# Local attention layers: half of the value windows used in place, tokens swapped on GpSimd, values and feed-forward part later

## What is computed

```python
def local_attention(q, k, v):            # 16 heads of 64, windows of 32 tokens
    bk2, bv2 = look(bk), look(bv)        # each window sees the one before and itself
    sim = einsum('bhwie,bhwje->bhwij', bq, bk2) * QK_SCALE
    attn = softmax(where(mask, -max, sim), -1)
    return einsum('bhwij,bhwje->bhwie', attn, bv2)
def attn_layer(x, Wqkv, qs, ksc, Wo):
    q, k, v = split(x @ Wqkv)            # q and k: l2norm, scale, rotary
    return local_attention(q, k, v) @ Wo
for i in range(6):
    x = attn_layer(shift_tokens(x), ...) + x
    x = ffn_layer(shift_tokens(x), ...) + x   # layernorm, W1, a * gelu(gate), W2
```

## Time and profile before

| | us |
|---|---|
| median of 3 runs | 2512.24 (2499.67 to 2514.59) |
| the profiled execution | 2506.73 |
| its span | 2504.8 |
| PE busy | 2354.9 |
| DVE busy | 1717.0 |
| ACT busy | 1597.2 |
| POOL busy | 1451.3 |

### The profile page before, as it was taken

How to read it: one execution, slowest core, us unless ns; L and a number is a source line. 1 busy time by engine, 2 the same in 40 slices (tenths; PEclk the granted TensorE clock), 3 DMA queues, 4 the chain that set the end, 5 groups by cost and what they waited for, 6 DMA issues and landing times.

```text
span 2504.8 us, 121652 instructions
## 1 busy us (share of the span) xinstructions
PE 2354.9 (94%) x53677; PEld 1748.5 (70%) x53677; DVE 1717.0 (69%) x3393; ACT 1597.2 (64%) x5036; POOL 1451.3 (58%) x1408
## 2 busy tenths in 40 slices
PE   9958999999999999999999999999888999999967
PEld 8836777777777777677777777777645666666657
DVE  4477788777888888787788788887335555555534
ACT  3226777777777787777777778777625454545422
POOL 1166667656676676566666677665117656656307
PEclk9969999999999999999999999999979999999978
DMA  4013333433333334333343333333216222222136
GB/s 91 15 33 86 79 83 94 97 80 83 91 93 95 82 83 103 83 92 87 80 96 90 80 92 87 87 87 87 54 30 177 49 48 48 48 48 48 31 97 249
DMA packets 230208, 204.60 MB, mean 82 GB/s; under 512 B 133687, under 2 KB 155464, under 8 KB 229552
## 3 DMA queue, kind: packets, MB, share of 16 engines
q1 hardware_dynamic: 225296, 190.91, 30.5%
q0 software_dynamic: 2208, 5.58, 0.7%
q10 hardware_dynamic: 2176, 0.33, 0.1%
HBM read 86.05 MB, written 15.70 MB: 41 GB/s over the span
## 4 chain that ended last, share of the span: by engine, by line
PE 66%; DVE 12%; SPq 6%; ACT 5%; issue 5%; POOL 4%; DMA 3%; POOLq 0%; ACTq 0%; DVEq 0%
PE psum L1211 7%; PE psum L1959 5%; PE psum L1237 5%; PE psum L1229 5%; PE psum L1938 4%; PE psum L1111 4%; PE psum L1944 3%; PE psum L1113 3%; PE psum L1112 3%; PE psum L1993 3%; PE psum L1983 3%; ACT p L1357 3%; SPq L972 3%; PE psum L1188 2%; PE psum L1219 2%
## 5 line engine op out<-in xcount | busy, mean ns | idle before, releaser
L1357 ACT ACTIVATE p<-p,stat 128x64 f32<-128x64 f32 x1536 | 512.4, 336 | 47.2 <-DVE stat L1491 44.9
L1577 POOL TENSOR_TENSOR p<-p,inverse 128x512 f32<-128x512 f32 x192 | 200.2, 1043 | 456.5 <-DVE inverse L1494 452.2
L1211 PE MATMUL psum<-kT,qT 32*32 32x64 f32 x24576 | 305.5, 224 | 25.8 <-issue 24.2
L2092 DVE TENSOR_REDUCE largest<-psum 128x1 f32<-128x512 f32 x256 | 165.0, 687 | 228.0 <-PE psum L1944 228.0
L1211 PEld LDWEIGHTS psum<-kT,qT 32*32 32x32 f32 x24576 | 264.1, 103 | 75.3 <-issue 74.3
L1357 ACT ACTIVATION_READ_ACCUMULATOR p<-p,stat 128x1 f32 x1536 | 288.6, 188 | 0.0
L1421 DVE SCALAR_TENSOR_TENSOR rotated<-psum,scales,rotary 128x512 f32<-128x512 f32 x384 | 270.8, 742 | 25.8 <-ACT sq L1293 25.8
L1556 POOL TENSOR_TENSOR squares<-sq 128x512 f32<-128x512 f32 x192 | 245.3, 1278 | 44.3 <-ACT sq L1293 43.8
L1293 ACT ACTIVATE sq<-psum 128x512 f32<-128x512 f32 x384 | 213.7, 582 | 57.3 <-PE psum L1113 54.6
L1229 PEld LDWEIGHTS psum<-pT,v_win 64*64 64x64 f32 x12288 | 198.6, 136 | 64.7 <-issue 45.9
L1111 PE MATMUL psum<-xs,wqkv_high 128*128 128x512 f32 x384 | 205.7, 536 | 23.2 <-DVE rotated L1421 22.9
(11 more groups left out here) (351 smaller groups left out, 5402.3 us busy)
## 6 DMA issues: line engine op xcount, KB each, us to landing
v_win<-v_tok SPq DMA_DIRECT2D x576, 128.0 KB
rnorm_wide<-rnorms SPq DMA_DIRECT2D x384, 64.0 KB
v_win<-v_tok SPq DMA_DIRECT2D x336, 64.0 KB
q_rows<-q_rows_all SPq DMA_DIRECT2D x32, 512.0 KB, 4.6
tile_weights<-expert_table SPq DMA_DIRECT2D x23, 512.0 KB, 5.8
wqkv<-L_ffn_Wqkv SPq DMA_DIRECT2D x96, 64.0 KB, 2.2
...
```

What stands on the lines that cost most here:

```text
L1211: last = PE.e.matmul(psum[WIN * blk:WIN * (blk + 1), f, out], q[rows, g, half, tok:tok + WIN], k[rows, g, half, tok:tok + 2 * WIN], start= ...
L1357: last = A.e.activation(p, p, ACT.Exp, bias=t.stat[:, h, 2 * g + f:2 * g + f + 1], accum_out=t.sum[:, h, g, f:f + 1])
L1577: G.e.tensor_tensor(p, p, t.inv[:, h, :, :].unsqueeze(3).to_broadcast([P, GROUPS_TF, 2, 2 * WIN]), ALU.mult).then_inc(*t.p_scaled.by(m))
L2092: V.e.tensor_reduce(t.mx[n % 4][:, :], psum[:, n % 5, :], AX, ALU.max, negate=True).then_inc(*t.largest.by(n))
```

## The change

Values. Windows 1 and 3 of a tile need the keys 0 to 63 and 64 to 127, which is how the copied values lie. `v_tok` goes; the copy writes slot 0 of `v_win`, used as it is for these two, and SP moves the data by 32 partitions into slot 1 for windows 0 and 2. So that f = 0 and f = 1 stay in different halves of the partitions, the tokens of the f = 1 values have their halves swapped: GpSimd makes a swapped copy `x_swapped` of the unit's tokens (two tensors, four copies of 128x256) at round 28, and the value matmuls of f = 1 use it. Score, weigh, mix and the norm copy follow that order; the norm copy becomes three instructions. DMAs per tile: 6 instead of 10 (4 instead of 8 in a unit's first). The value copy now waits for the weighing of the tile two before.

Schedule. Values from round 29 to 33, windows from 31 to 37, the whole feed-forward part four rounds later, the norms' row out at 19 instead of 15, wide norms at 20, 20, 26, 29 instead of 16, 18, 19, 24, and the loads of the next layer's weights two rounds later. The windows of a round now stand before its wide norms in SP's queue.

```diff
-VALUE_FIRST, WINDOWS_AT = 29, 31
+VALUE_FIRST, WINDOWS_AT, SWAP_AT = 33, 37, 28
...
-NORM_AT = {"root0": 17, "out": 15, "root1": 33, "turn": 39, "copy": 39}
-SPREAD_AT = (16, 18, 19, 24)
-SCALE_AT = (24, 28, 29, 32)
+NORM_AT = {"root0": 17, "out": 19, "root1": 33, "turn": 39, "copy": 39}
+SPREAD_AT = (20, 20, 26, 29)
+SCALE_AT = (24, 28, 31, 32)
-FFN_AT = {"shift": 80, "center": 83, "square": 84, "sum": 84, "root": 84, "spread": 88, "scale": 89, "gate0": 91, "gate1": 95, "gate2": 96, "gelu": 99,
-          "up0": 100, "up1": 101, "up2": 104, "down": 108, "add": 109}
+FFN_AT = {"shift": 84, "center": 87, "square": 88, "sum": 88, "root": 88, "spread": 92, "scale": 93, "gate0": 95, "gate1": 99, "gate2": 100, "gelu": 103,
+          "up0": 104, "up1": 105, "up2": 108, "down": 112, "add": 113}
...
+SPLIT_AT = {2: 13, 3: 31, 0: 39, 1: 40, 4: 60, 5: 62}
...
+                if s == PART_FIRST + PART * (PARTS - 1) + PART_STEPS + 1:
...
-            if s in SPREAD_AT:
-                norms_wide(c, t, u, SPREAD_AT.index(s))
             i, at = divmod(s - WINDOWS_AT, TILE)
             if 0 <= i < TPB and at == 0:
                 value_windows(c, t, u * TPB + i)
+            for g in range(GROUPS_TF):
+                if s == SPREAD_AT[g]:
+                    norms_wide(c, t, u, g)
     for v_in in t.v_in + t.wide_in:
...
+def swapped(f, blk):
+
+    return f if blk < TPB // 2 else 1 - f
...
+    w0, w1, w2, w3 = (slice(WIN * w, WIN * (w + 1)) for w in range(TPB))
+    SP.e.dma_start(v[WIN:P, 1, 0, :, :], v[0:P - WIN, 0, 0, :, :]).then_inc(*v_in.by((n, 0)))
+    SP.e.dma_start(v[w1, 1, 1, :, :], v[w0, 0, 1, :, :]).then_inc(*v_in.by((n, 1)))
+    SP.e.dma_start(v[w0, 1, 1, :, :], v[w3, 0, 1, :, :]).then_inc(*v_in.by((n, 2)))
+    SP.e.dma_start(v[w3, 1, 1, :, :], v[w2, 0, 1, :, :]).then_inc(*v_in.by((n, 3)))
+    if n % TPB:
+        SP.e.dma_start(v[w0, 1, 0, :, :], before[w3, 0, 0, :, :]).then_inc(*v_in.by((n, 4)))
+        SP.e.dma_start(v[w2, 1, 1, :, :], before[w1, 0, 1, :, :]).then_inc(*v_in.by((n, 5)))
...
+        if f:
+            PE.wait_ge(*t.swapped.on(u))
+        tokens = [x[:, i * P:(i + 1) * P] for x in (t.xp if f else xs)]
+        three_products(PE, ps, tokens, w).then_inc(*t.valued.by((u * TPB + i, f)))
...
+def mixed_rows(t, h, g):
+
+    ot = t.ot[h][:, g, 0:H64]
+    return bass.AP(ot.tensor, ot.offset, [list(ot.ap[0]), [P + H64 if g % 2 == 0 else H64 - P, 2], [1, H64]])
...
-                        last = PE.e.matmul(psum[WIN * blk:WIN * (blk + 1), f, out], q[rows, g, half, tok:tok + WIN], k[rows, g, half, tok:tok + 2 * WIN],
+                        last = PE.e.matmul(psum[WIN * blk:WIN * (blk + 1), swapped(f, blk), out], q[rows, g, half, tok:tok + WIN], k[rows, g, half, tok:tok + 2 * WIN],
...
-        PE.wait_ge(*t.v_in[n % 2].on((n, 9 if i else 7)))
+        PE.wait_ge(*t.v_in[n % 2].on((n, 5 if i else 3)))
         for a in range(2):
             for blk in range(TPB):
                 for o in range(2):
                     for f in range(2):
-                        rows, to, at = slice(DH * f, DH * f + DH), (f + o) % 2 * DH, a * P + blk * WIN
-                        last = PE.e.matmul(psum[to:to + DH, 2 + o, at:at + WIN], v[rows, blk, 2 * (2 * a + o) + h, :],
+                        slot, to, at = swapped(f, blk), (f + o) % 2 * DH, a * P + blk * WIN
+                        rows = slice(DH * slot, DH * slot + DH)
+                        last = PE.e.matmul(psum[to:to + DH, 2 + swapped(o, blk), at:at + WIN], v[rows, 1 - blk % 2, f, 2 * (2 * a + o) + h, :],
                                            t.pt[h][rows, 2 * a + o, blk * WIN:(blk + 1) * WIN], start=True, stop=True)
         last.then_inc(*t.weighted.by(m))
...
+def swap_halves(t, u, k):
+
+    to, x = (y[:, :].rearrange("p (i a q) -> p i a q", i=TPB, a=2) for y in (t.xp[k], t.xs[u % 2][k]))
+    return [(to[:, :, 1 - a, :], x[:, :, a, :]) for a in range(2)]
...
-        A.e.activation(t.rq[u % 2][:, :, :].rearrange("p b r -> p (b r)"), ring_bank(c, t, "unit", u, "rn")[:, 0:P], ACT.Copy).then_inc(*t.rn_kept.by(u))
+        norms = ring_bank(c, t, "unit", u, "rn")[:, 0:P]
+        A.e.activation(t.rq[u % 2][0:H64, :, :].rearrange("p b r -> p (b r)"), norms[0:H64, :], ACT.Copy)
+        pairs = lambda x: x.rearrange("p (b a h f g) -> p b a h f g", b=TPB, a=2, h=2, f=2)
+        for f in range(2):
+            last = A.e.activation(pairs(t.rq[u % 2][H64:P, :, :].rearrange("p b r -> p (b r)"))[:, :, 1, :, 1 - f, :], pairs(norms[H64:P, :])[:, :, 1, :, f, :], ACT.Copy)
+        last.then_inc(*t.rn_kept.by(u))
...
-        for m in (n - 2, n - 1):
-            if m >= 0:
-                A.wait_ge(*t.v_in[m % 2].on((m, 9 if m % TPB else 7)))
-        A.e.activation(t.vt[n % 2][:, f, :, 0:DH], ring_bank(c, t, "unit", u, f"v{i}{f}").rearrange("p (h d) -> p h d", d=DH), ACT.Copy).then_inc(*t.v_kept.by((n, f)))
+        if n >= 2:
+            A.wait_ge(*t.weighted.on(2 * (n - 2) + 1))
+        if n >= 1:
+            A.wait_ge(*t.v_in[(n - 1) % 2].on((n - 1, 5 if (n - 1) % TPB else 3)))
+        A.e.activation(t.v[n % 2][:, 0, f, :, :], ring_bank(c, t, "unit", u, f"v{i}{f}").rearrange("p (h d) -> p h d", d=DH), ACT.Copy).then_inc(*t.v_kept.by((n, f)))
...
+    if s == SWAP_AT:
+        if u:
+            G.wait_ge(*t.valued.on((u * TPB - 1, 1)))
+        for k in range(2):
+            for to, x in swap_halves(t, u, k):
+                last = G.e.tensor_copy(to, x)
+        last.then_inc(*t.swapped.by(u))
```

More of the change, by code:

```diff
@@ L726 @@
 TABLES = (2, 3, 0, 1)
-UNIT_STEPS = 110
-SPLIT_AT = {2: 13, 3: 31, 0: 39, 1: 40, 4: 56, 5: 59}
+UNIT_STEPS = 118
+SPLIT_AT = {2: 13, 3: 31, 0: 39, 1: 40, 4: 60, 5: 62}
 RAW = 2
@@ L790, in transformer_setup @@
     t.xs = [[sb(f"xs{i}_{k}", [P, S], F32R) for k in range(2)] for i in range(2)]
+    t.xp = [sb(f"x_swapped{k}", [P, S], F32R) for k in range(2)]
     t.xf = sb("x_ffn", [P, S])
@@ L799, in transformer_setup @@
     t.rq = [sb(f"rnorm_tok{i}", [P, TPB, 32]) for i in range(2)]
-    t.vt = [sb(f"v_tok{i}", [P, 2, PAIRS, DH]) for i in range(2)]
-    t.v = [sb(f"v_win{i}", [P, TPB, PAIRS, DH]) for i in range(2)]
+    t.v = [sb(f"v_win{i}", [P, 2, 2, PAIRS, DH]) for i in range(2)]
     t.stat, t.sum, t.inv = sb("stat", [P, 2, 2 * GROUPS_TF]), sb("sum", [P, 2, GROUPS_TF, 2]), sb("inverse", [P, 2, GROUPS_TF, 2])
@@ L819, in transformer_setup @@
     t.valued, t.v_kept = per("valued", tiles, halves), per("v_kept", tiles, halves)
-    t.v_in = [Signal(nc, f"tf_v_in{i}", [(n, k) for n in range(i, UNITS_TF * TPB, 2) for k in range(10 if n % TPB else 8)], 16) for i in range(2)]
+    t.v_in = [Signal(nc, f"tf_v_in{i}", [(n, k) for n in range(i, UNITS_TF * TPB, 2) for k in range(6 if n % TPB else 4)], 16) for i in range(2)]
     t.scored, t.scores_kept, t.biased, t.exped, t.inverted, t.p_scaled, t.turned, t.pt_kept, t.weighted, t.o_kept = (
@@ L828, in transformer_setup @@
     t.shift_high, t.shift_low = per("shift_high", units, halves), per("shift_low", units, halves)
+    t.swapped = one("swapped", units)
     t.tab_turned, t.tab_kept = one("tables_turned", TABLES), one("tables_kept", TABLES)
@@ L925, in transformer_sync @@
             if b == B - 1 and l + 1 < DEPTH:
-                if s == PART_FIRST + PART * (PARTS - 1) + PART_STEPS - 1:
+                if s == PART_FIRST + PART * (PARTS - 1) + PART_STEPS + 1:
                     SP.wait_ge(*t.mixed.on((u + 1) * TPB - 1))
                     load_mix(c, t, l + 1)
-                if s == FFN_AT["add"]:
+                if s == FFN_AT["add"] + 2:
                     SP.wait_ge(*t.f_down.on(u))
@@ L933, in transformer_sync @@
                     then, after = (l + 1, x + RAW) if x + RAW < len(SPLIT_AT) else (l + 2, x + RAW - len(SPLIT_AT))
-                    if s == SPLIT_AT[k] + 1 and then < DEPTH:
+                    if s == SPLIT_AT[k] + 3 and then < DEPTH:
                         SP.wait_ge(*t.split_low.on((l + 1, k)))
@@ L960, in value_windows @@
 def value_windows(c, t, n):
-    SP, v, vt, v_in = c.SP, t.v[n % 2], t.vt[n % 2], t.v_in[n % 2]
+    SP, v, before, v_in = c.SP, t.v[n % 2], t.v[(n - 1) % 2], t.v_in[n % 2]
     SP.wait_ge(*t.v_kept.on((n, 1)))
@@ L967, in value_windows @@
         SP.wait_ge(*t.weighted.on(2 * (n - 2) + 1))
-    k = 0
-    for f in range(2):
-        at = f * 2 * WIN
-        for blk in range(1, TPB):
-            SP.e.dma_start(v[at:at + 2 * WIN, blk, :, :], vt[(blk - 1) * WIN:(blk + 1) * WIN, f, :, :]).then_inc(*v_in.by((n, k)))
-            k += 1
-        SP.e.dma_start(v[at + WIN:at + 2 * WIN, 0, :, :], vt[0:WIN, f, :, :]).then_inc(*v_in.by((n, k)))
-        k += 1
-        if n % TPB:
-            SP.e.dma_start(v[at:at + WIN, 0, :, :], t.vt[(n - 1) % 2][P - WIN:P, f, :, :]).then_inc(*v_in.by((n, k)))
-            k += 1
+    w0, w1, w2, w3 = (slice(WIN * w, WIN * (w + 1)) for w in range(TPB))
[6 more added lines that the diff above has]
+        SP.e.dma_start(v[w2, 1, 1, :, :], before[w1, 0, 1, :, :]).then_inc(*v_in.by((n, 5)))
```

(7 more changed lines are left out.)

2 lines of the change are left out of this document (1 added, 1 removed).

## The result

The changed kernel takes 2686.93 us (median, 2685.00 to 2701.67) against 2510.60 us for the kernel before on the same chip: ratio 1.0722, with an interval of 1.0671 to 1.0774. The forecast was 2553 us in a range that ended at 2592. It went the way that I had forecast, but by almost four times as much (176 us in place of 46). The profiled execution took 2685.0 us.

A forecast was written before the change was run, and what follows sets the result against it. The prediction took TensorE to bound the kernel, busy 342 of 350 us in the layers. Its terms, 37 + 17 + 4 + 3 - 15 = +46 us on 2507, gave 2553 us, range 2500 to 2592.

The forecast's parts named there:

- three stalls: New TensorE waits: norms' copy behind the GELUs 37 us, square before the feed-forward sum 17, second up product 4.
- What it takes away: Fewer window-copy DMAs in SP's queue, so value copies and TensorE wait less: 15 us gained, bounds 5 and 35.
- GpSimd's four copies: Swap copies at round 28, 1.6 us per unit, hidden in GpSimd's idle time before the scaling: 0 us.
- without that cover 38 us: Cost of GpSimd's swap copies if no idle time hid them: 24 x 1.6 = 38 us.
- Weighing: Block changes in TensorE's new weighing order cost nothing or one 18 ns slot each, up to 10 us; 3 taken.
- The loads stand free: Rival, chance 0.03: at each weighing block change a 136 ns weight load waits; 78 us in place of 3, 2628 us.
- Centre and sum: TensorE's feed-forward norm sum waits for ScalarE's square, 0.74 us in 23 units: 17 us, bounds 12 and 23.
- GELU and norms: GELUs delay ScalarE's norm copy to 5.3 us after score start S; TensorE's sum of squares stalls 1.7 us, 22 times: 37.
- up1 wait: TensorE's second up product waits for its bank behind VectorE's late score copy: 0 to 0.4 us each, 4 us taken.
- The clock: Rival, chance 0.07: each new 1.7 us stall also costs 1.3 us of granted clock, 29 us more, 2582 us.
- The list of neighbours: Check of what the feed-forward part, moved four rounds against the attention's parts, newly stands beside; it priced two places.
- Two places matter: Claim that the moved feed-forward part meets trouble only at centre with sum, and at GELU with norms.

The follow-up runs named there:

- e13_no_swap: The changed kernel without the four GpSimd swap copies and without the wait for them; ratio 1.051 to the kernel before.
- e10_only_later: The kernel before with only the new rounds: values and feed-forward part four rounds later, last two weight splits at 60 and 62; ratio 1.061.
- e6_centre_earlier: The changed kernel with the feed-forward centre at round 85 instead of 87 and its square at 86 instead of 88; ratio 1.079 to the kernel before.

## Why the prediction was wrong

The direction was right, and the three stalls that it named are there. But the sum was 46 us and should have been 176, and the three are the smaller part: 35.7 us of TensorE's 125.6 us of idle time between 350 and 1750 us. Moving two of them away gained nothing. So that the direction came out is in part luck. By its own steps:

- **What it takes away, 15 us**: right in kind, and somewhat more. No value copy waits for a DMA any more, where the earlier trace rows had 27.7 us, and the bytes fall from 204.60 to 154.22 MB. Layout without swap against the place alone, e13_no_swap to e10_only_later, is 1.0505 / 1.0607 = 0.990, some 25 us gained; the two extra norm copies and the new places of the norms are in this number too.
- **GpSimd's four copies, 0 us**: wrong, and the first failed step. They cost 2.1%, some 50 us. I took the cover from the mean idle time before the scaling, 2.7 us, and read it as room at round 28. But the shift, 1.27 + 1.09 us, stands at the same round behind the copies, and a mean over 169 waits says nothing about the one round. The trace of the kernel before had the answer: of 20 scalings behind a shift between 350 and 1750 us, 8 had no idle time ahead of them and 11 had 1.34 us. One of the 8:

```profile
1049.80 1.96 POOL L1542 TENSOR_TENSOR xs<-z,xs 64x511 fp32r<-64x511 f32 x1
1051.84 1.04 POOL L1577 TENSOR_TENSOR p<-p,inverse 128x512 f32<-128x512 f32 x1
```

  And beside VectorE's key scaling the four copies take 2.62 us, as in the unit shown, and not 1.6 (2.33 on average). My own "without that cover 38 us" was nearer. The Trainium skill ("SBUF — State Buffer", section "Who interferes with whom") says that a VectorE instruction with two SBUF inputs contends with a GpSimd instruction that reads SBUF. The trace agrees: of 96 copies the median is 398 ns and the longest 1468.
- **Weighing, 3 us**: nothing of it is seen, and it is small either way. The 64 instructions take 1.14 us in the median as before; the mean of one is 226 ns against 221, at a clock that is 4 to 5% lower. "The loads stand free" is refuted: three loads of 136 ns standing free would have made 1.14 us into 1.55.
- **Centre and sum, 0.74 us**: right, 14.0 us in 19 waits. But with the centre and its square earlier (e6_centre_earlier) the wait went and no time was won, so mending this wait alone doesn't give back its 17 us.
- **GELU and norms, 1.7 us**: right mechanism, size off: 17.2 us in 17 waits, 1.0 each, mostly 1.15. In the unit at 1247 us:

```profile
1241.98 1.22 PE L1224 MATMUL psum<-kT,qT 32*32 32x64 f32 x103
1243.62 0.43 PE L1224 MATMUL psum<-kT,qT 32*32 32x64 f32 x25 [0.42 <-issue]
...
1247.08 0.64 PE L1146 MATMUL psum<-squares,onehot 128*32 128x128 f32 x16 [0.78 <-ACT rnorm_tok L1322]
...
1249.18 1.13 PE L1190 MATMUL psum<-sq,w 128*128 128x512 f32 x2 [0.35 <-DVE act L1490]
```

  The norms are kept at S + 5.1 (I had S + 5.3), and TensorE would have come at 1246.30, S + 4.3 (I had 3.57), of which 0.42 are an "issue" wait in the score matmuls. The up1 wait is 0.35, within my 0 to 0.4.
- **The clock, nothing in the sum and 29 us as a rival**: wrong, the second failed step. 2.3 us a unit, 55 us. I had asked what a single stall of 1.7 us does, not what a unit with eight of them does.
- **The list of neighbours**: wrong, the third failed step and the largest. "Two places matter" looks only at what the moved part itself waits for or holds up. The new place also puts the part's copies and scalings among other work on ScalarE and VectorE, takes the value matmuls away from ahead of a turn on TensorE, and puts a weight split ahead of GpSimd's squares. In the place alone the waits that I had not priced are 53 us in 1400, for 24 units of 73.7 us 53 x 1769 / 1400 = 67 us, not in my sum at all; the three that I had priced are 32 x 1769 / 1400 = 40 us there. Its clock costs 1.5 us a unit, 37 us. I had priced the deadlines that the moved instructions miss themselves, not those missed by what stands behind them, though the profile said how little slack TensorE had.

The range went wrong with these: its upper end added up the bounds of steps that I had, and no rival held a loss on GpSimd or by many small waits.
